# Attention on one Trainium2 core: the softmax shifts of both key tiles of a group as four products on quarters of the array's rows, ahead of the score parts

## The reference, cut to what matters

```python
x = x + _L0_attn_ref(_layernorm(x), ...)        # 16 heads of 64, 1024 keys
x = x + _L0_xattn_ref(_layernorm(x), ctx, ...)  # 16 heads of 64, 6404 keys
x = x + _L0_ffn_ref(_layernorm(x), ...)
x = x + _L1_attn_ref(_layernorm(x), ...)        # 16 heads of 8, rotary, 1024 keys
x = x + _L1_xattn_ref(_layernorm(x), ctx, ...)  # 8 heads of 64, 6404 keys
x = x + _L1_ffn_ref(_layernorm(x), ...)
# in each attention, for each head:
attn = softmax(q @ k.T * scale)
out = attn @ v
```

## Time and profile before

| what | us |
|---|---|
| median of 3 runs | 4618.46 |
| lowest and highest run | 4615.41, 4620.7 |
| the profiled execution's own time | 4600.18 |
| its span, first to last instruction | 4598.4 |
| PE busy | 4301.6 (94%) |
| weight loads (PEld) busy | 2382.7 (52%) |
| POOL busy | 3141.8 (68%) |
| DVE busy | 2227.8 (48%) |
| ACT busy | 1803.9 (39%) |

### The profile page before, as it was taken

The page is one execution under the profiler, slowest core; times in us unless marked ns, Lnnn a source line. Parts: engine busy times, 40 slices in busy tenths (PEclk is TensorE's granted clock), DMA queues, the critical chain, the costliest instruction groups (busy, mean ns, idle before and its releaser), DMA issues. The chain is left out here.

```text
span 4598.4 us, 69354 instructions
## 1 busy us (share of the span) xinstructions
PE 4301.6 (94%) x25904; PEld 2382.7 (52%) x25904; DVE 2227.8 (48%) x2764; ACT 1803.9 (39%) x2082; POOL 3141.8 (68%) x1379
## 2 busy tenths in 40 slices
PE   7999799999999999999999968599899999999968
PEld 3555455555555555555555446244455555555436
DVE  4555655555454555555455112456565545455212
ACT  2333244444444444444444422133234444444422
POOL 3556279989898988989899930000048989899950
PEclk9999899999999999999999979799779999999979
DMA  1000000000000000000000001100000000000001
GB/s 34 5 5 2 4 2 1 2 2 2 2 2 2 2 2 2 3 2 2 2 1 2 1 17 46 40 9 12 4 1 2 2 2 1 1 1 2 1 12 30
DMA packets 30387, 30.95 MB, mean 7 GB/s; under 512 B 6929, under 2 KB 22786, under 8 KB 30082
## 3 DMA queue, kind: packets, MB, share of 16 engines
q1 hardware_dynamic: 28626, 24.39, 1.8%
q10 hardware_dynamic: 1456, 2.46, 0.2%
HBM read 23.17 MB, written 3.67 MB: 6 GB/s over the span
## 5 line engine op out<-in xcount | busy, mean ns | idle before, releaser
L410 POOL TENSOR_TENSOR c_SUM<-c_SUM,c_PR 128x1024 f32<-128x1024 f32 (+1 forms) x1176 | 2792.9, 2375 | 263.9 <-ACT c_PR L490 158.7
L568 DVE TENSOR_REDUCE c_MX<-c_XB 128x2 f32<-128x1024 f32 (+2 forms) x1156 | 1394.3, 1206 | 1224.0 <-PE c_XB L690 1223.0
L490 ACT ACTIVATE c_PR<-c_S 128x1024 f32<-128x1024 f32 (+1 forms) x1224 | 1194.7, 1023 | 1694.9 <-PE c_S L735 1579.8
L753 PE MATMUL c_O<-c_PR,c_V 128*64 128x512 f32 (+1 forms) x4896 | 1197.0, 607 | 2.8 <-ACT c_PR L490 2.8
L753 PEld LDWEIGHTS c_O<-c_PR,c_V 128*64 128x64 f32 (+1 forms) x4896 | 294.0, 136 | 568.4 <-issue 394.1
L735 PE MATMUL c_S<-c_SH,c_ONE 64*128 64x512 f32 x2448 | 482.0, 389 | 0.0
L490 ACT ACTIVATE a_PR<-a_S 128x1024 f32<-128x1024 f32 x256 | 248.7, 1022 | 444.9 <-PE a_S L735 444.9
L568 DVE TENSOR_REDUCE a_MX<-a_XB 128x2 f32<-128x1024 f32 x246 | 301.2, 1224 | 188.0 <-PE a_XB L690 96.6
L690 PE MATMUL c_XB<-c_KHM,c_QH 64*128 64x512 f32 x1632 | 369.5, 448 | 11.7 <-DVE c_MX L568 7.7
L735 PE MATMUL c_S<-c_QH,c_KHM 64*128 64x512 f32 x1728 | 348.3, 399 | 8.5 <-ACT c_PR L490 8.4
L735 PE MATMUL c_S<-c_QH,c_KLM 64*128 64x512 f32 x1728 | 341.5, 391 | 0.0
(11 more groups left out here) (209 smaller groups left out, 4352.7 us busy)
## 6 DMA issues: line engine op xcount, KB each, us to landing
f_W<-in_L_w SPq DMA_DIRECT2D x34, 256.0 KB, 2.7
CTX<-in_ctx ACTq DMA_DIRECT2D x12, 192.0 KB, 4.4
a_KS<-scratch_k SPq DMA_DIRECT2D x16, 96.0 KB
a_QS<-scratch_q SPq DMA_DIRECT2D x16, 96.0 KB
scratch_q<-rot_qh SPq DMA_DIRECT2D x2, 512.0 KB, 4.6
scratch_k<-rot_kh SPq DMA_DIRECT2D x2, 512.0 KB, 6.2
c_WQ<-in_L_xattn_Wq SPq DMA_DIRECT2D x12, 64.0 KB, 1.8
c_WO<-in_L_xattn_Wo SPq DMA_DIRECT2D x12, 64.0 KB, 1.8
```

The costliest lines, as they stand in the source:

```text
L410: pool.tensor_tensor(out[0:kp], out[0:kp], tile[0:kp], ALU.add).then_inc(summed, 1)
L490: act.activation(PR[u % BUFS][0:kp, :, :].rearrange("p h q -> p (h q)"), S[u % 2][0:kp, :], ACT.Exp)\
L568: dve.tensor_reduce(MX[:, q:q + tiles, :, column], bank[:].rearrange("p (h k) -> p h k", h=2) [:, :, 0:tiles * m].rearrange("p h (q k) -> ...
L753: last = pe.matmul(O[ROWS[h], :], V[pair.par][0:kp, t, ROWS[h]], PR[u % BUFS][0:kp, h, :], start=t == 0, stop=t == TILES - 1)
```

## The change

The shift of a tile is no longer the last term of its scores. A new `shifts` on PE goes ahead of the scores of a group and does the shifts of both tiles and both heads, each as a product on 32 rows: head 0 of the first tile on rows 0 to 31, head 1 of the first tile on rows 64 to 95, then rows 32 to 63 and 96 to 127 for the second tile. It starts the accumulation in the two S buffers, and the other terms add to it. For that SH holds each shift twice (rows 0 and 32, rows 64 and 96): DVE's reduction reads MX twice through a stride of zero and writes columns 0 and 32 of NM. ONE has four rows of ones (0, 32, 64, 96), so FILLS goes up by two. The waits move with the shifts: both S buffers of the group must be free before the first shift.

```diff
-        FILLS = 5 + (4 if packed is None and TILES * P > keys else 0 if packed is None else 12)
+        QUARTERS = [slice(32 * i, 32 * i + 32) for i in range(4)]
+        FILLS = 7 + (4 if packed is None and TILES * P > keys else 0 if packed is None else 12)
...
-                fill(ONE[0:1, :].bitcast(F32), 1.0)
-                fill(ONE[64:65, :].bitcast(F32), 1.0)
+                for rows in QUARTERS:
+                    fill(ONE[rows.start:rows.start + 1, :].bitcast(F32), 1.0)
...
                     dve.wait_ge(x_free, count)
-                    dve.tensor_reduce(NM[:, :, :, 0], MX[:], AX.X, ALU.max, negate=True).then_inc(shift_ready, 1)
+                    twice = MX[:].rearrange("p q h c -> p (q h) c").unsqueeze(2)\
+                        .broadcast_to([P, 8, 2, plan.columns])
+                    out = NM[:].rearrange("p q h e -> p (q h) e")[:, :, 0:E:E // 2]
+                    dve.tensor_reduce(out, twice, AX.X, ALU.max, negate=True).then_inc(shift_ready, 1)
...
-                def scores(pair, half, t, end):
-                    u = half * TILES + t
-                    g = plan.step(pair.p, half, t)
-                    if t == 0:
+                def shifts(pair, half, group, end):
+
+                    steps = steps_of(group)
+                    if group == 0:
...
-                    if not (pair.first and u < 2):
-
-                        pe.wait_ge(p_done, g - 1)
+                    if not (pair.first and half == 0 and group == 0):
+
+                        pe.wait_ge(p_done, plan.step(pair.p, half, steps[-1]) - 1)
+                    for i, t in enumerate(steps):
+                        for h in range(2):
+                            rows = QUARTERS[2 * h + i]
+                            pe.matmul(S[(half * TILES + t) % 2][:, h * 512:(h + 1) * 512], ONE[rows, :], SH[half][rows, :],
+                                      start=True, stop=False)
+
+                def scores(pair, half, t):
+                    u = half * TILES + t
...
-                    terms.append((ONE[:], SH[half][:]))
...
-                                             start=i == 0, stop=i == len(terms) - 1)
+                                             start=False, stop=i == len(terms) - 1)
...
                             maxima(0)
+                            shifts(pair, half, group, end)
                             for t in steps_of(group):
-                                scores(pair, half, t, end)
+                                scores(pair, half, t)
```

## The result

The changed kernel takes 4734.2 us in the median of four runs (4726.68 to 4738.11) against 4617.07 us for the kernel before (four runs). The ratio is 1.0251, 95% interval 1.0233 to 1.0268: slower by 117 us, where 110 was forecast (4728 us). The profiled execution took 4738.11 us with a span of 4736.3.

A forecast was written before the change was run, and what follows sets the result against it. PE was taken to bound ten of twelve pairs of c0 and c1. 93 + 2 + 10 + 3 + 1.4, about +110 us, gave 4710 on the profiled execution, 4728 for the median; range 4595 to 4805.

The forecast's parts named there:

- The price of a switch: On PE between XB, shifts and S: each change between 64 and 32 rows costs 0.20 us (0.09 drain, 0.11 load).
- One slot for four quarters: In the shift group on PE: four quarter products run together in one slot of 0.23 us.
- c0 and c1, 93 + 2 us: Ten PE-bound pairs, 9.3 us each, add 93 us; the last pairs, before POOL saturates, add 2 us.
- a0 and a1, 10 + 3 us: 0.17 us in each of 60 groups of a0 and in 16 of a1 without a second XB.
- The later first tile: S for a group's first tile ends 0.40 us later, so ACT and POOL get it later; costs nothing.
- Reduction, fills, moved wait: DVE's doubled reduction (0.12 us more in c) and the moved wait cost nothing; two more fills per attention, 1.4 us altogether.
- idle time of PE behind ACT ahead of the shifts: Sign that the prediction is wrong: the moved wait for both S buffers would hold up PE.
- The rival without a switch: 64 to 32 rows costs nothing; each group saves 0.23 us, about 115 us together, 4503 us; chance 0.14.
- reserve for POOL: In that rival, POOL's hand-overs and waits at the half's turn limit ten pairs' saving to 70 to 115 us.

The follow-up runs named there:

- the twins: Two runs: kernel before plus a pair of 4-column products ahead of each group's first score tile, on 32 or on 64 rows; 4861.97 and 4666.24 us.
- halves by tile: Changed kernel with shifts on 64 rows, each tile's shift right ahead of that tile's terms with its own wait; 4609.93 us against 4607.31, ratio 1.0007.
- a0 and a1 in old form: Changed kernel with the shift again last term on 64 rows in attentions a0 and a1; 4708.96 us against 4609.24, ratio 1.0209.
- tiny on 32 rows: Kernel before plus a pair of 4-column products on 32 rows ahead of each group's first score tile; 4861.97 us, ratio 1.054.
- tiny on 64 rows: Kernel before plus a pair of 4-column products on 64 rows ahead of each group's first score tile; 4666.24 us, ratio 1.0107.
- halves first: Changed kernel with the shifts still first, but on 64 rows for each head (two slots); 4626.86 us against 4610.54, ratio 1.0032.
- a1 in old form: Changed kernel with the shift again last term on 64 rows in attention a1 alone; 4743.12 us, ratio 1.0286.
- one slot less: Kernel before with shifts first on 64 rows and each group's second tile's shift left out; 4478.02 us against 4610.54, ratio 0.9708.
- quarters ahead of XB: Changed kernel with the shifts ahead of the first XB, behind O, instead of behind XB; 4769.58 us, ratio 1.0357.
- two quarters: Changed kernel with the second tile's two quarter products left out of each group; 4770.27 us, ratio 1.0354.

## Why the prediction was right

The forecast was 4728 with a range of 4595 to 4805, the result 4734.2. Point by point:

- *The price of a switch*, taken from changes between 64 rows and the full array because no row showed one between 64 and 32: right to 0.01 us in each distance, and shown by the twins (196 us for rows alone). The Trainium skill, TensorEngine Tiling (Array Packing), Key Properties, has a drain at each change of tiling mode; the traces agree for 64 and 32 rows, and show 0.09 to 0.10 us until the old products are out, and 0.11 for a load that nothing covers.
- *One slot for four quarters*: right (0.43 with two and with four, which leaves 0.23 for the slot). The Trainium skill, TensorE: Matmul & The Clock Gate, Measured speedup vs the span model, has 3.07 times for four row tiles; the estimate from it, a slot of 0.30 and 4768 us, isn't borne out here.
- *c0 and c1, 93 + 2 us*: right. From POOL's first addition of a pair of c0 to that of the next it was 263.5 us in the middle before and 273.0 after: +9.5, forecast 9.3. The 265.1 named in the prediction is the mean of two pairs of 263.4 and 266.9 us, the longest of the seven among them, so its 274 came out 1 us too high. The last pair of c0 stayed hidden behind POOL: from its first addition to the layer norm behind c0 it was 265.9 us before (2437.03 to 2702.92) and 266.7 after (2524.43 to 2791.15).
- *a0 and a1, 10 + 3 us*: right for the work, and too low for the stages; 25 us on the chip where both forms ran. What failed is the clock: the sum took it from the kernel before, 1.00 to 0.97, and had no term for its falling. At equal clock a0 cost 10 us and a1 no more than 3, as the table of products shows; a0 ran at 0.95 and 0.94 instead of 0.97, a1 at 0.87 and 0.89 instead of 0.91. Why the clock fell in a0 is not shown. The later first tile, costed at nothing ("O of that tile is a group away"), has a small price: that step looked at PE's product and not at ACT, which has the side jobs behind exp. It is seen as 1.4 us in a0, and the two runs with the shifts first on 64 rows put it, together with the moved wait, at some 9 us.
- *Reduction, fills, moved wait*: the run by tile had the first two for nothing that can be measured. The prediction named idle time of PE behind ACT ahead of the shifts as a sign of being wrong, and the changed kernel has 31.7 us of it in c. But it all lies in the two last pairs, 15.8 us and 16 waits in each, where POOL adds without a pause and the S terms of the kernel before waited too (20.0 us in all); in the ten full pairs there is none. So the moved wait cost those pairs nothing. The line is that of the last pair of c0 (2524 to 2790): time waited, number of waits, the longest.

```profile
PE c_S L731 <- ACT c_PR L491: 15.8, 16, 1.1
```

- *The rival without a switch* was priced at 115 us with a reserve for POOL; the run of that price gave 133, and c0 and c1 alone 111.9 where 97 had been counted. The reserve was wrong: POOL's lag of one half is paid back in the next.
- *Luck*: the two profiled executions, from which the rows are read, differ by 138 us, 28 more than the sum, and a0 and a1 account for it. That the medians differ by 117, within 7 us of the sum, is partly luck: the profiled execution of the kernel before lay 17 us under its median and that of the changed one 4 above.

## What to carry to other kernels

Products of another row count in the middle of a run of matmuls cost two edges, however little they compute; weigh that against the slots saved by the distance from start to start at an edge that the trace already has. By these distances products on quarters can be worth it only where several slots of them stand together, or where an edge is there anyway and nothing behind it has a wait that runs out too early; no run here had such a place. A tile that is finished later delays not only its reader but everything queued behind that reader. And before a stage's extra time is put down to a mechanism, its granted clock has to be read beside it.

## What the runs showed of the hardware that was not expected

The clock of a stage can fall while PE hardly waits. Most groups of a1 are bound by DVE's 1.83 us between two XB, and PE's longest wait in its pairs was 0.4 us before and 0.3 us after. The granted clock in those pairs, one trace each (1.00 is 2.4 GHz throughout, less means time at 1.2 GHz in between):

| kernel | clock in the pairs of a1 |
|---|---|
| before; halves by tile; a0 and a1 in old form; tiny on 32 rows; tiny on 64 rows | 1.00 |
| halves first | 0.99 |
| a1 in old form | 0.98 |
| changed, two traces | 0.95, 0.98 |
| one slot less, all on 64 rows | 0.96 |
| quarters ahead of XB | 0.89 |
| two quarters | 0.87 |

Two pairs of neighbours say that leaving products out goes with a lower clock: from halves first to one slot less, where nothing else changes, 0.99 to 0.96, and from four quarters to two, 0.95 and 0.98 to 0.87. Adding tiny products left it at 1.00. So leaving out products could make the kernel slower: two quarters took 4770.27 us where four took 4734. It isn't the whole story: with a1 in its old form and nearly the work of the kernel before it was 0.98, the quarters ahead of XB leave out nothing against the changed kernel and still had 0.89, and a0, where PE is the bound, ran lower with quarters too. How much PE must do in which time isn't told by these runs.

The clock also moved without a change of the work. At the start of c0 stand projections; in the first 83 us of them the kernel before ran at 0.86, the run with the halves by tile at 0.50, 1.2 GHz throughout:

```profile
507.00:590.00 83.00, 64.47 (x272) 33.85 (x272) 69.66 (x71) 18.13 (x31) 0.48 (x3) 0.86 0.02 5
```

```profile
512.00:595.00 83.00, 78.23 (x216) 40.06 (x216) 61.92 (x60) 15.52 (x26) 1.24 (x7) 0.50 0.02 4
```

The second got 216 matmuls done in the time in which the first did 272. From the layer norm to POOL's first addition c0 took 90.6 us in the kernel before (499.81 to 590.43) and 105.2 in the run with the halves by tile (505.29 to 610.53). That is why c0 is 12 to 15 us longer in the stage table for runs whose time is close to that of the kernel before. The changed kernel shows both cases: 90.8 us at the start of c0 and 105.4 at that of c1 in its first trace, 105.4 and 90.8 in its second, whose c0 is 15 us longer and whose c1 is 17 us shorter. So a stage of a single trace is good to some 15 us only; differences below that were read from start to start within a group, from pair to pair of c0, or from the ratio over all runs.
